# Loading Wq and Wk by head at the start of an attention and MoE kernel, and handing head 0's split to three engines

## The reference

```python
mod = (silu(c) @ wmod)                      # sa, ca, ga, sb, cb, gb: six rows of 256 per batch
h = layernorm(x) * (1 + ca) + sa
q, k, v = (h @ (codes * repeat(scales, 32, axis=0)) + b for q, k, v)   # 256 -> 16 heads of 128
attn = softmax(q @ k.T / sqrt(128)); o = attn @ v                      # per batch and head
x = x + ga' * (o @ Wo + bo)                 # ga' keeps its sign and is at least 0.25 in size
h = layernorm(x) * (1 + cb) + sb
x = x + gb' * (h @ W.T + lora(h))           # 8 LoRA experts of rank 16, the best 2 per token
```

## Time and profile before

| what | us |
|---|---|
| median of 3 runs | 777.8 (777.14 to 778.07) |
| the profiled execution: its own time | 777.42 |
| its span, first to last instruction | 775.5 |
| TensorE busy (PE) | 766.5 (99%) |
| VectorE busy (DVE) | 647.5 (83%) |
| ScalarE busy (ACT) | 517.6 (67%) |
| GpSimd busy (POOL) | 483.4 (62%) |
| mean granted clock of TensorE | 0.998 |

### The profile page before, as it was taken

How to read it: one execution, slowest core, us unless ns; L and a number is a source line. 1 busy time by engine, 2 the same in 40 slices (tenths; PEclk the granted TensorE clock), 3 DMA queues, 4 the chain that set the end, 5 groups by cost and what they waited for, 6 DMA issues and landing times.

```text
span 775.5 us, 14722 instructions
## 1 busy us (share of the span) xinstructions
PE 766.5 (99%) x4206; PEld 667.7 (86%) x4206; DVE 647.5 (83%) x1254; ACT 517.6 (67%) x1124; POOL 483.4 (62%) x454
## 2 busy tenths in 40 slices
PE   7999999999999999999999999999999999999998
PEld 6888888888888888888888888888888888888887
DVE  5889888888888888888888888888898888879876
ACT  2788676667666676667666766676667676766841
POOL 4686576548655675556657575655667476789722
PEclk9999999999999999999999999999999999999999
DMA  7554355444454335444445434543355334433202
GB/s 216 162 154 124 95 147 150 139 107 99 118 144 131 95 96 139 129 124 98 110 133 147 98 94 122 146 125 95 96 145 152 95 94 107 112 89 86 56 1 109
DMA packets 71898, 90.67 MB, mean 117 GB/s; under 512 B 19574, under 2 KB 37431, under 8 KB 71867
## 3 DMA queue, kind: packets, MB, share of 16 engines
q1 hardware_dynamic: 53184, 74.00, 37.3%
q10 hardware_dynamic: 18682, 16.30, 7.0%
HBM read 22.06 MB, written 2.11 MB: 31 GB/s over the span
## 4 chain that ended last, share of the span: by engine, by line
PE 95%; POOL 1%; DVE 1%; DMA 1%; ACT 1%; SPq 1%; issue 0%; DVEq 0%
PE score L1102 9%; PE score L1103 9%; PE score L1104 9%; PE qv L1102 8%; PE qv L1103 8%; PE qv L1104 8%; PE o L1102 7%; PE o L1104 7%; PE o L1103 7%; PE ky L1102 4%; PE ky L1103 4%; PE ky L1104 4%; PE y L1102 2%; PE y L1104 2%; PE y L1103 2%; DMA stage<-in_L_attn_wk_scales_dram 1%
## 5 line engine op out<-in xcount | busy, mean ns | idle before, releaser
L404 POOL TENSOR_TENSOR pT_lo<-pT,pT_hi 128x512 fp32r<-128x512 f32 x248 | 314.6, 1305 | 240.7 <-ACT pT_hi L576 240.6
L660 ACT ACTIVATE prob<-score,neg_max 128x512 f32<-128x512 f32 x256 | 172.7, 688 | 79.7 <-DVE neg_max L941 79.5
L941 DVE TENSOR_REDUCE neg_max<-score 128x1 f32<-128x512 f32 x256 | 159.7, 682 | 1.6 <-PE score L1104 1.6
L954 DVE STREAM_TRANSPOSE pB<-prob 128x512 f32<-128x512 f32 x252 | 156.4, 678 | 0.0
L576 ACT ACTIVATE pT_hi<-pT 128x512 fp32r<-128x512 f32 x248 | 135.3, 620 | 0.0
L1102 PE MATMUL score<-k_hi,q_hi 128*128 128x512 f32 x256 | 101.2, 395 | 0.6 <-DVE k_lo L862 0.6
L1103 PE MATMUL score<-k_lo,q_hi 128*128 128x512 f32 x256 | 100.3, 392 | 0.0
L1104 PE MATMUL score<-k_hi,q_lo 128*128 128x512 f32 x256 | 99.7, 389 | 0.0
L1102 PE MATMUL o<-pT_hi,v_hi 128*128 128x512 f32 x248 | 96.6, 389 | 0.0
L1104 PE MATMUL o<-pT_hi,v_lo 128*128 128x512 f32 x248 | 96.5, 389 | 0.0
L1103 PE MATMUL o<-pT_lo,v_hi 128*128 128x512 f32 x248 | 96.5, 389 | 0.0
(11 more groups left out here) (262 smaller groups left out, 1824.7 us busy)
## 6 DMA issues: line engine op xcount, KB each, us to landing
pT<-pB SPq DMA_DIRECT2D x1008, 64.0 KB, 2.0
out_dram<-x_nat SPq DMA_DIRECT2D x8, 256.0 KB, 2.1
stage<-in_L_attn_wv_codes_dram ACTq DMA_DIRECT2D x7, 256.0 KB
stage<-in_L_attn_wv_scales_dram ACTq DMA_DIRECT2D x14, 128.0 KB
stage<-in_L_attn_wq_codes_dram ACTq DMA_DIRECT2D x7, 256.0 KB
stage<-in_L_attn_wq_scales_dram ACTq DMA_DIRECT2D x14, 128.0 KB
stage<-in_L_attn_wk_codes_dram ACTq DMA_DIRECT2D x7, 256.0 KB
stage<-in_L_attn_wk_scales_dram ACTq DMA_DIRECT2D x14, 128.0 KB
```

Source lines behind the costliest of these rows:

```text
L404: pool.tensor_tensor(split(pT_lo, kt), turned(par, kt), split(pT_hi, kt).bitcast(f32), ALU.subtract).then_inc(p_lo_ok, 1)
L660: act.activation(prob[:, i], score_ps[i][:, :], ACT.Exp, bias=neg_max[:, i:i + 1], accum_out=row_sum[:, s % 2, i:i + 1]).then_inc(exp_ok, 1)
L941: dve.tensor_reduce(neg_max[:, i:i + 1], score_ps[i][:, :], AX.X, ALU.max, negate=True).then_inc(max_ok, 1)
L954: dve.transpose(pB[:, s % 2, :, i].rearrange("p g k q -> p k g q"), prob[:, i].rearrange("p (k g q) -> p k g q", k=QT, g=G)).then_inc(pB_o ...
```

## The change

- Wq and Wk of the first pair are loaded by head (`load_head`): one DMA for the codes of a head and four for its scales. SP issues head 0 of q, head 0 of k, x of batch 1, v, head 1 of q, head 1 of k, and then the rest as before.
- VectorE makes both products for q and k, head by head (`head_product`, 128 x 2 x 128). Those of head 1 stand after `k_low(1)` and the variances of batch 1. GpSimd no longer makes k's product.
- Head 0's parts: GpSimd makes both of q, ScalarE w_hi of k, VectorE w_lo of k. ScalarE also makes hT_hi of batch 0's second half.
- GpSimd's order is then q's head 0, the product and parts of v, `inverse_std(1)` (the power alone), the parts of q's head 1, the parts of k's head 1.
- Batch 1: its statistics are split in two by `q_low(1)`, its variances come after `k_low(1)`, and its z is made by VectorE, after unit 0's four maxima, and no longer by ScalarE. In unit 0 `q_low` for unit 1 comes before the third and fourth transposes, not after.
- The bias vectors are transposed before `transpose_input(0)`, and ScalarE, not VectorE, copies them, before hT32 of batch 0.
- 14 fillers become 5 (before q's projection), 10 become 8 (after k's).

```diff
-            load_first(sp, "q")
-            load_first(sp, "k")
+            load_head(sp, "q", 0)
+            load_head(sp, "k", 0)
             load_x(1)
             load_first(sp, "v")
+            load_head(sp, "q", 1)
+            load_head(sp, "k", 1)
             load_x(2)
...
+        def load_head(queue, m, j):
+            cols = slice(j * HD, (j + 1) * HD)
+            queue.dma_start(codes[m][:, :, cols], CODES[m].rearrange("(c p) f -> p c f", p=P)[:, :, cols]).then_inc(ld_head[m][j], 16)
+            for a in range(NB):
+                src = bass.AP(SCALES[m].tensor, a * FEAT + j * HD, [[0, BLK], [NB * FEAT, 2], [1, HD]])
+                queue.dma_start(scales[m][BLK * a:BLK * (a + 1), :, cols], src).then_inc(ld_head[m][j], 16)
... GpSimd
             inverse_std(0)
             parts("q", 0, 0)
-            product("k", 0)
-            parts("k", 0, 0)
-            parts("q", 0, 1)
-            inverse_std(1)
             product("v", 0)
             parts("v", 0, 0)
+            inverse_std(1)
+            parts("q", 0, 1)
             parts("k", 0, 1)
... ScalarE
+            act.wait_ge(vec_tr, 1)
+            act.activation(vecT[:, NH:VECS], o_ps[1][:, NH:VECS], ACT.Copy).then_inc(vec_ok, 1)
+            act.activation(vecT[:, 0:NH], o_ps[1][:, 0:NH], ACT.Copy, scale=SCORE_SCALE).then_inc(vec_ok, 1)
+            act.wait_ge(vec_ok, 2)
+            act.activation(bias_now[:, 0:2], bias[:, 0:2, 0:2], ACT.Copy).then_inc(bias_ok, 1)
             act.wait_ge(mod_ok, 2)
...
             for c in range(DC):
                 input_high(0, c, score_ps[2 + c])
-            act.wait_ge(vec_ok, 2)
-            act.activation(bias_now[:, 0:2], bias[:, 0:2, 0:2], ACT.Copy).then_inc(bias_ok, 1)
+            act.wait_ge(h_ev, 2)
+            act.activation(hT_hi[:, 1, tokens(0)], hT32[:, 1], ACT.Copy).then_inc(h0_hi, 1)
+            act.wait_ge(w_half["k"], 1)
+            act.activation(w_hi["k"][head_cut(0)], w32["k"][head_cut(0)], ACT.Copy).then_inc(w_hi_ok["k"], 1)
...
             q_high(1, 0)
             k_high(1, 0)
-            normalise(1, range(QT))
... VectorE
-            dve.wait_ge(ld_w_first["q"], LDW_FIRST)
-            dve.scalar_tensor_tensor(out=w32["q"][:, :, :], in0=codes["q"][:, :, :], scalar=SCORE_SCALE, in1=scales["q"][:, :, :],
-                                     op0=ALU.mult, op1=ALU.mult).then_inc(w_prod["q"], 1)
-            for c in range(DC):
-                input_hi(0, c)
-                input_lo(0, c)
-            dve.wait_ge(vec_tr, 1)
-            dve.tensor_copy(vecT[:, NH:VECS], o_ps[1][:, NH:VECS]).then_inc(vec_ok, 1)
-            dve.tensor_scalar(vecT[:, 0:NH], o_ps[1][:, 0:NH], SCORE_SCALE, None, ALU.mult).then_inc(vec_ok, 1)
+            def head_product(m, j):
+                dve.wait_ge(ld_head[m][j], LDW_FIRST)
+                cut = head_cut(j)
+                dve.scalar_tensor_tensor(out=w32[m][cut], in0=codes[m][cut], scalar=SCORE_SCALE if m == "q" else 1.0,
+                                         in1=scales[m][cut], op0=ALU.mult,
+                                         op1=ALU.mult).then_inc(w_prod[m] if j else w_half[m], 1)
+            head_product("q", 0)
+            head_product("k", 0)
+            input_hi(0, 0)
+            input_lo(0, 0)
+            input_lo(0, 1)
+            dve.wait_ge(w_hi_ok["k"], 1)
+            dve.tensor_tensor(w_lo["k"][head_cut(0)], w32["k"][head_cut(0)], w_hi["k"][head_cut(0)].bitcast(f32),
+                              ALU.subtract).then_inc(w_ok["k"], 1)
             dve.wait_ge(vec_ok, 2)
             dve.wait_ge(ld_x[1], 16)
-            statistics(1)
+            row_statistics(1, 0)
+            row_statistics(1, 1)
...
             q_low(1, slice(0, 1))
+            row_statistics(1, 2)
+            row_statistics(1, 3)
             k_low(1, slice(0, 1))
+            variances(1)
+            head_product("q", 1)
+            head_product("k", 1)
...
                     maximum(3)
+                    if start:
+                        normalise(1)
...
                         if start:
                             v_low(1, 0, 0, ky_ps)
+                            q_low(n + 2, head_slice(p, s + 1))
                         turn(2)
                         turn(3)
...
-                        q_low(n + 2, head_slice(p, s + 1))
+                        if not start:
+                            q_low(n + 2, head_slice(p, s + 1))
... TensorE
-            transpose_input(0)
             pe.wait_ge(ld_vec, 16 * 3)
             pe.transpose(o_ps[1][:, 0:VECS], vec_raw[:, :], ident[0:VECS, 0:VECS]).then_inc(vec_tr, 1)
-            for i in range(14):
+            transpose_input(0)
+            for i in range(5):
...
-            for i in range(10):
+            for i in range(8):
```

More of the change, by code:

```diff
@@ L186, in bass_adaln_mxfp4_attention_moe_lora_kernel @@
         ld_w = {m: sem(f"ld_w{m}") for m in "qkvo"}
-        ld_w_first = {m: sem(f"ld_w{m}_first") for m in "qkvo"}
+        ld_w_first = {m: sem(f"ld_w{m}_first") for m in "vo"}
+        ld_head = {m: [sem(f"ld_head_{m}{j}") for j in range(2)] for m in "qk"}
+        w_half, h0_hi = {m: sem(f"w{m}_half") for m in "qk"}, sem("h0_hi")
         c_exped, silu_step, mod_mm, mod_ok = (sem(n) for n in ("c_exped", "silu_step", "mod_mm", "mod_ok"))
@@ L282, in load_first @@
             if m == "o":
-                rows = CODES[m].rearrange("(h p) d -> p h d", p=P)[:, 0:2]
-                at, row, half = [BLK * a for a in range(NB)], D, NB * D
-            else:
-                rows = CODES[m].rearrange("(c p) f -> p c f", p=P)[:, :, 0:PW]
-                at, row, half = [BLK * a for a in range(NB)], FEAT, NB * FEAT
+                rows, row, half = CODES[m].rearrange("(h p) d -> p h d", p=P)[:, 0:2], D, NB * D
+            else:
+                rows, row, half = CODES[m].rearrange("(c p) f -> p c f", p=P)[:, :, 0:PW], FEAT, NB * FEAT
             queue.dma_start(codes[m][:, :, :], rows).then_inc(ld_w_first[m], 16)
@@ L290, in load_first, with head_cut @@
                 src = bass.AP(SCALES[m].tensor, a * row, [[0, BLK], [half, 2], [1, PW]])
-                queue.dma_start(scales[m][at[a]:at[a] + BLK], src).then_inc(ld_w_first[m], 16)
+                queue.dma_start(scales[m][BLK * a:BLK * (a + 1)], src).then_inc(ld_w_first[m], 16)
+        def load_head(queue, m, j):
[4 more added lines that the diff above has]
+                queue.dma_start(scales[m][BLK * a:BLK * (a + 1), :, cols], src).then_inc(ld_head[m][j], 16)
+        def head_cut(j):
+            return slice(None), slice(None), slice(j * HD, (j + 1) * HD)
         def split(t, kt):
@@ L386, in parts @@
                     cut, done = (slice(None), slice(None), slice(j * HD, (j + 1) * HD)), 2 * p + j
-                pool.wait_ge(w_prod[m], p + 1)
+                if isinstance(p, int) and p == 0 and m in "qk" and j == 0:
+                    pool.wait_ge(w_half[m], 1)
+                else:
+                    pool.wait_ge(w_prod[m], p + 1)
                 pool.tensor_tensor(w_hi[m][cut], w32[m][cut], one[:, 0:1].to_broadcast([P, PW]) if m == "o" else ones[:, 0:1].to_broadcast([P, 2, HD if m in "qk" else PW]), ALU.mult).then_inc(w_hi_ok[m], 1)
@@ L393, in input_lo @@
                 for c in range(DC):
-                    if b < 2:
-                        pool.wait_ge(h_hi, DC * b + c + 1)
+                    if b == 1:
+                        pool.wait_ge(h_hi, c + 2)
                     else:
@@ L813, in input_lo @@
             def input_lo(b, c):
-                dve.wait_ge(h_hi, DC * b + c + 1)
+                if c:
+                    dve.wait_ge(h0_hi, 1)
+                else:
+                    dve.wait_ge(h_hi, 1)
                 dve.tensor_tensor(hT_lo[:, c, tokens(b)], hT32[:, c], hT_hi[:, c, tokens(b)].bitcast(f32),
@@ L1121, in transpose_input @@
             def transpose_input(b):
-                if b == 0:
-                    pe.wait_ge(z_ok, QT)
+                if b < 2:
+                    pe.wait_ge(z_ok, QT * (b + 1))
                 else:
-                    pe.wait_ge(zin_ok, QT * b)
+                    pe.wait_ge(zin_ok, QT * (b - 1))
                 banks = INPUT_BANKS[b]
@@ L1243, in ffn_input @@
                 else:
-                    pe.wait_ge(z_ok, QT * 2)
+                    pe.wait_ge(z_ok, QT * 3)
                 if b:
```

10 lines of the change are left out of this document (5 added, 5 removed).

## The result

The kernel with the change took 781.41 us (median of 5 runs, 778.75 to 783.70) against 777.80 (777.14 to 778.41) before, a ratio of 1.0048 with a 95% interval of 1.0034 to 1.0061. The forecast was 777.4 with a range of 775.4 to 779.9: it missed on the slow side. The profiled execution of the changed kernel took 778.75 us and is the fastest of its five, so it shows 1.3 us of the loss and not the median's 3.6.

A forecast was written before the change was run, and what follows sets the result against it. The start of unit 0's scores and of k's projection in unit 1 were taken to bound the kernel. Saving 2.3 us and giving back 1.35 + 0.5 made -0.4 on the 777.8 median: 777.4 us, range 775.4 to 779.9.

The forecast's parts named there:

- What bounds the kernel: TensorE hardly waits after the first scores, so moving them (20.43 us) moves the end, unless new waits appear.
- Loads: First heads of q and k, half the bytes: k's taken to land at 11.5 us, ends 10.7 and 13.9.
- rival C: k's head lands late, at 13.0, and second heads' loads too: net +1.7, 779.5; 781 or more at 13.9. Chance 0.18.
- estimate of 10.7: Landing of k's head if 512 B transfers reach line rate; the sum would be the same.
- The order and length of VectorE's chain in unit 0: Second heads' products, maxima, z, transposes, v_lo: 7.6 us, 1.35 more; TensorE waits about 2 before k of unit 1.
- The price of meeting GpSimd: VectorE beside GpSimd in unit 0: 0.5 us, between nothing and 2.4, with GpSimd free by 20 us.
- The bound of 2.4 us: Most the meeting could cost: addition up to 1.29, k's product 1.00, z for the rest.
- The sentence by the Trainium skill's rule: Shared ports held per whole instruction: the power holds k's product 1.0 us, making the sum 0.5 worse.
- rival D: Meetings of VectorE and GpSimd in unit 0 cost their upper bound: 778.9 us. Chance 0.15.
- A: The forecast itself: 2.3 us saved, 1.35 and 0.5 given back; between -1.3 and +0.4. Chance 0.42.
- The clock: Same clock at same times: two or three of q's matmuls at 0.43 us, others 0.23; nothing for the gap.
- Rival B: An earlier start, k landed by 10.7, full clock for q, no meeting with GpSimd: 775.7 us. Chance 0.25.

The follow-up runs named there:

- look2: The changed kernel, unaltered, profiled once more in a single run: 781.68 us.
- look1: The changed kernel, unaltered, profiled once more in a single run: 783.42 us.
- look3: The changed kernel, unaltered, profiled once more in a single run: 783.49 us.
- fill_both: The changed kernel with 14 and 10 fillers around the first projections again and 26 more before TensorE's wait for v_lo: 780.39 us, ratio 1.0039.
- apart_12: The changed kernel with GpSimd's parts of k's head 1 held until z is made, and 12 and 12 fillers: 778.72 us, ratio 1.0015.
- after_again: The changed kernel, unaltered, timed in five more runs and profiled: median 782.30 us, ratio 1.0062; profiled execution 779.79 us.
- after: The first profiled execution of the changed kernel: 778.75 us.
- whole_loads: The changed kernel with q and k of the first pair loaded whole again, products still by head: 783.43 us, ratio 1.0068.
- fill_start: The changed kernel with 14 fillers ahead of q's projection and 10 behind k's, as before the change: 781.21 us, ratio 1.0049.
- pool_apart: The changed kernel with GpSimd's parts of k's head 1 held until VectorE's four z are made: 778.78 us, ratio 1.0010.

## Why the prediction was wrong

*What bounds the kernel*: right. What happens before the first scores moves the end one for one, and the place where VectorE can hold TensorE again was k's projection of unit 1, by v_lo.

*Loads*: mis-sized. k's head was taken to land at 11.5 with 10.7 and 13.9 as ends; it landed at 12.51 to 13.14. The fastest execution started its scores at 18.81, not 18.15, and saved 1.6, not 2.3. That is near rival C's landing of 13.0, and C's late loads of the second heads came true in look2 (0.74 us). The prediction's estimate of 10.7, from the Trainium skill's minimum of 512 B for line rate (DMA: Bandwidth & Descriptors, Specifications), was the farthest off: rows of 512 B landed 1.8 us later than that, or more.

*The order and length of VectorE's chain in unit 0*: right in kind. Second heads' products, maxima, z, transposes and v_lo stood in that order, the maxima began 1.8 us behind the scores (over 2 was said), and the wait before k of unit 1 was put down to v_lo, at 3.45 where about 2 was said.

*The price of meeting GpSimd*: the term that failed first. It was set at 0.5, nearer to nothing, because GpSimd was to be free by 20 us. GpSimd was through with v at 19.99, almost as said, but then came the power, the second heads' splits and the product of o, 5.4 us without a gap, exactly under z. The bound of 2.4 us was all but reached (2.3 by length, 2.0 on the path), but that the figures agree is luck: its parts were 1.29 for the addition, 1.00 for k's product behind the power and the rest, 0.1, for z, and the runs show 0.85, nothing and 1.5. The sentence by the Trainium skill's rule, that the power on four columns would hold k's product for its whole length, did not come true: the product took 0.42 us beside it. Against before, from unit 0 to 1 the profiled execution gave back 2.87 us and not 1.85. This is rival D's price (1.3 to 1.9 more than A) with a smaller saving; the two give the +1.3 us of the profiled execution.

*The clock*: the step that turned a small loss into the miss. "A gap to 13.1, for which I count nothing" is the cut of the fillers, and the wait of about 2 us before k of unit 1 was counted by its length alone. The first cost up to 2.5 us and the second up to 2.8, in look1 and look3 both together (4.0 and 4.8); with both places filled, the spread fell from 3.6 to 0.8 us. Rival C had the mechanism, but tied it to a late landing and priced three matmuls at 0.6 us; with k landing at 13.14, near where it had it, twelve matmuls were hit in look1. That a wait which the change itself makes lowers the clock behind it was in no case.

*Not foreseen and not settled*: the waits of weight loads for pT_lo, about 1 us in fill_both and apart_12; and what sets the times of executions apart that have the same mean clock.

How the median's loss divides can only be estimated. In the five profiles of the change the clock cost 0, 1.4, 1.6, 4.0 and 4.8 us, 2.4 on average, and without it they would lie 0.9 to 2.6 us above the 777.42 of the kernel before. The difference of the ratios of after_again and fill_both gives 1.8 for the clock, which is too little, since fill_both had about 1 us of waits for pT_lo that the change has not, and 0.55 us of the clock in its own profile. Rival B's early start without a meeting was never seen.

## What to carry to other kernels

Before moving an instruction from an idle engine to a busy one, lay the other engines' timelines beside its new place: z held nobody up on ScalarE in the kernel before, and took VectorE 1.66 us, or 3.16 beside GpSimd. A bound on such a meeting is worth little if its parts are put on the wrong instructions. A wait or a cut filler on TensorE has two prices, its length and what the lower clock takes from the matmuls behind it; the second comes in some executions only, so it shows in the median and the spread and may be absent from the one profile. When the profiled execution is at the edge of its runs, profile again before explaining the median.

## What the runs showed of the hardware

- A VectorE instruction on four columns took 1.02 us beside wv_lo and 0.17 us in look1 with GpSimd waiting; four z of 128x256 took 3.16 to 3.22 us against 1.66. In look2 the z took 2.85 and the addition 1.15. A product of 128x256 that began 0.2 us behind GpSimd's power on four columns (1.12 us) took 0.42 us, no longer than alone.
- The same kernel's TensorE ran the same twelve matmuls of q and k at 0.23 us apart in one execution and at 0.43 in another, with 0.6 us between the starts of the projection (14.15 in after, 14.78 in look1). In look2 they started at 14.76 and ran at 0.23.
- At the wait before k of unit 1, of 3 to 4 us, the clock fell to 0.50 in look1, look2, look3 and whole_loads (2.99), in its last microsecond or up to 1 us behind it, and did not in after (3.45), after_again (2.95) or fill_start (3.12). With 1.4 and 2.2 us (pool_apart, apart_12) it did not in the one profile of each.
- In fill_both the clock was at 0.50 from 8.7 to 15.5 us, with TensorE at work without a break from 9.66 on.
- The landing of the same first loads differed by 0.6 us between the five profiled executions of the changed kernel (12.51 to 13.14), and by 1.3 us over all fourteen profiles that load by head (12.03 to 13.35).
